# Attention with a compressive memory and an fp8 layer on one core: the order of the units in an even head, and the row tiles of the third strips

## The reference, cut to what matters

```python
# x: (2, 2048, 512); 4 query groups, 8 heads, 16 elements a head
x = layernorm(L0_attn_x)
q, k, v = x @ Wq.T, x @ Wk.T, x @ Wv.T
scores = einsum('bsqhd,bthd->bqhst', qh, kh) / sqrt(16)
a_dot = einsum('bqhst,bthd->bsqhd', softmax(scores), vh)
sigma_q = elu(q.reshape(b, s, 4, 128))
a_mem = sigma_q @ memory / (sigma_q @ memory_norm)
x1 = L0_attn_x + a_dot * (1 - w) + a_mem * w          # w = sigmoid(memory_weight)
out = x1 + fp8(layernorm(x1) / input_scale) * input_scale @ (weight * weight_scale).T
```

## Time and profile before

| | |
|---|---|
| median of 3 runs | 1942.49 us (1942.41 to 1942.53) |
| the profiled execution | 1942.58 us |
| span from its first to its last instruction | 1940.5 us |
| ACT busy | 1833.6 us, 94% of the span |
| PE busy | 1863.9 us, 96% |
| DVE busy | 1409.9 us, 73% |
| granted TensorE clock | 1.000 |

### The profile page before, as it was taken

The page is one execution under the profiler, slowest core; times in us unless marked ns, Lnnn a source line. Parts: engine busy times, 40 slices in busy tenths (PEclk is TensorE's granted clock), DMA queues, the critical chain, the costliest instruction groups (busy, mean ns, idle before and its releaser), DMA issues.

```text
span 1940.5 us, 115379 instructions
## 1 busy us (share of the span) xinstructions
PE 1863.9 (96%) x54988; PEld 1162.0 (60%) x54996; DVE 1409.9 (73%) x1833; ACT 1833.6 (94%) x1596; POOL 107.2 (6%) x150
## 2 busy tenths in 40 slices
PE   8999999999999999999999999999999999999998
PEld 7885555556565555555555555555655555555555
DVE  6675777777777777787777777777777777777755
ACT  5556999999999999999999999999999999999997
POOL 5541000000000000000000000000000000000000
PEclk9999999999999999999999999999999999999999
DMA  6654111121112211222112211212112211222111
GB/s 220 201 187 153 54 54 40 45 57 45 54 41 56 78 49 42 56 58 64 47 49 56 78 47 44 57 46 76 44 53 57 78 50 41 56 50 72 43 47 46
DMA packets 131327, 130.38 MB, mean 67 GB/s; under 512 B 30451, under 2 KB 106455, under 8 KB 130855
## 3 DMA queue, kind: packets, MB, share of 16 engines
q1 hardware_dynamic: 129847, 121.15, 21.2%
q10 hardware_dynamic: 1008, 1.84, 0.3%
HBM read 86.96 MB, written 32.24 MB: 61 GB/s over the span
## 4 chain that ended last, share of the span: by engine, by line
ACT 76%; PE 21%; issue 2%; DVE 1%; POOL 0%; DMA 0%; ACTq 0%; DVEq 0%; POOLq 0%
ACT pool L865 74%; PE ps L1153 8%; PE ps L945 6%; PE ps L1028 4%; ACT pool L872 1%; PE ps L1200 1%; PE ps L918 1%; DMA resid<-in_x 0%; PE ps L984 0%; POOL q_sq L727 0%; PE ps L909 0%; POOL xn L704 0%; PE ps L926 0%; DVE v_tiles L1608 0%; DVE v_tiles L1610 0%
## 5 line engine op out<-in xcount | busy, mean ns | idle before, releaser
L865 ACT ACTIVATE pool<-ps 128x1536 f32<-128x1536 f32 (+1 forms) x1388 | 1710.1, 1413 | 17.0 <-PE ps L1028 14.7
L1153 PE MATMUL ps<-pool,v_st 64*32 64x128 f32 (+2 forms) x35744 | 1398.3, 357 | 14.7 <-issue 13.7
L1153 PEld LDWEIGHTS ps<-pool,v_st 64*32 64x32 f32 x35744 | 854.5, 106 | 210.0 <-issue 54.3
L1028 PE MATMUL ps<-q_st,k_st 51*32 51x512 f16 x16128 | 903.6, 381 | 49.0 <-ACT pool L865 11.6
L1028 PEld LDWEIGHTS ps<-q_st,k_st 51*32 51x32 f16 x16128 | 246.0, 89 | 474.3 <-ACT pool L865 427.5
L1593 DVE TENSOR_SCALAR late<-ps 128x512 int32<-128x512 f32 x248 | 171.6, 692 | 212.5 <-PE ps L1028 212.5
L1608 DVE SCALAR_TENSOR_TENSOR v_tiles<-late 128x2048 f32<-128x2048 f32 x62 | 142.1, 2293 | 148.1 <-PE ps L1153 144.7
L1612 DVE SCALAR_TENSOR_TENSOR pool<-v_tiles,late 128x2048 f32<-128x2048 f32 x62 | 142.1, 2292 | 2.1
L1610 DVE SCALAR_TENSOR_TENSOR v_tiles<-v_tiles,late 128x2048 f32<-128x2048 f32 x62 | 142.1, 2292 | 2.1
L1603 DVE SCALAR_TENSOR_TENSOR late<-late 128x2048 f32<-128x2048 f32 x62 | 141.6, 2285 | 0.0
L747 POOL TENSOR_TENSOR rstd<-var_eps,minus_half 128x1 f32<-128x1 f32 x32 | 23.0, 720 | 1696.8 <-DVE var_eps L1672 1696.8
(11 more groups left out here) (169 smaller groups left out, 955.1 us busy)
## 6 DMA issues: line engine op xcount, KB each, us to landing
v_st<-v_aug SPq DMA_DIRECT2D x64, 256.0 KB, 3.5
q_st<-q_aug SPq DMA_DIRECT2D x127, 128.0 KB
k_st<-k_aug SPq DMA_DIRECT2D x127, 128.0 KB
sigma_kept<-y_out SPq DMA_DIRECT2D x32, 256.0 KB, 2.0
q_aug<-parts SPq DMA_DIRECT2D x32, 256.0 KB, 2.7
wqT<-sigma_kept SPq DMA_DIRECT2D x32, 256.0 KB, 3.8
q_st<-q_aug SPq DMA_DIRECT2D x127, 64.0 KB
k_st<-k_aug SPq DMA_DIRECT2D x127, 64.0 KB
```

The costliest lines, as they stand in the source:

```text
L865: act.activation(probs[:, u % HELD, 0:UNITS[u].width * CH], scored(u).rearrange("p a b -> p (a b)"), ACT.Exp, bias=LIFT, scale=EXP_UNIT / ...
L1028: return pe.matmul(ps[VW * c:VW * c + VW, bank, :], k_st[RT * r:RT * r + AUG, n % 2, keys:keys + VW], q_st[RT * r:RT * r + AUG, n % 2, q * ...
L1153: last = pe.matmul(acc[r][VW * c:VW * c + VW, :].rearrange("v (i s) -> v i s", s=VW)[:, places, :], v_st[rows, n % 2, j, :], by_place[rows ...
```

## The change

Three edits:

1. In an even head the two narrow units with the memory products move from places 0 and 2 to places 3 and 5. The head still has 22 units, 16 wide and 6 narrow, and its late units stay at places 10 to 13. The memory products now use the other third bank (odd units instead of even ones). `WEIGHED_LATER` stays as it was.
2. The row tile in which each half of a third strip runs now changes with every unit, instead of every second one.
3. VectorE takes and adds the sums of the head before first, and then adds both memory products.

```diff
-UNITS_OF_HEAD = (["2memory", "3", "2memory"] + ["3"] * 7 + ["2late"] * 4 + ["3"] * 8,
+UNITS_OF_HEAD = (["3", "3", "3", "2memory", "3", "2memory"] + ["3"] * 4 + ["2late"] * 4 + ["3"] * 8,
                  ["3", "3", "2product", "3", "2spare", "3", "3"] + ["2late"] * 4 + ["3"] * 11)
 WEIGH_BEHIND = 2
 WEIGHED_LATER = ((0, 1, 2), (0, 1, 2, 3, 9))
@@
             def third_scores(u, n, strip):
                 for c in range(P // VW):
-                    last = strip_scores(THIRD_BANK[u % SLOTS], n, strip, (c // 2 + u // 2) % ROW_TILES, c)
+                    last = strip_scores(THIRD_BANK[u % SLOTS], n, strip, (c // 2 + u) % ROW_TILES, c)
                 return last
@@
             def head(n):
                 g, h = divmod(n, HEADS)
+                if n > 0:
+                    take_sums(n - 1)
+                    add_sums(n - 1)
                 if n % 2 == 0:
                     add_memory(n)
-                if n > 0:
-                    take_sums(n - 1)
-                if n % 2 == 0:
                     add_memory(n + 1)
-                if n > 0:
-                    add_sums(n - 1)
                 if n % 2 == 0:
                     if g > 0:
                         tile_moments((g - 1) * TPC + h // 2)
```

## The result

The changed kernel takes 1969.91 us (median of four runs, 1963.16 to 1973.21) where the kernel before takes 1942.51 (four runs). The ratio is 1.0135, 95% interval 1.0107 to 1.0162. It is slower, by 27.4 us; the forecast was 1969.2 us. The profiled execution took 1969.06 us, of which 1967.0 are span.

A forecast was written before the change was run, and what follows sets the result against it. ScalarE was taken to set the pace, TensorE following with a small reserve. A net loss of 0.83 us in each of 32 even heads gives +26.6 us on 1942.58, other terms cancelling: 1969.1 to 1969.2 us, 8-in-10 range 1963 to 1975.

The forecast's parts named there:

- The path through turns 3 to 6: Even heads, unit 1's end to unit 6's end: TensorE's path takes 6.85 us where ScalarE alone needs 5.86.
- The losses: ScalarE's delay per even head: 0.14 us at unit 4 and 0.85 at unit 6, net 0.83 us a head.
- Unit 1's 0.16: Even heads of the kernel before: memory products at place 0 cost 0.16 us, 5.1 us in all, which the change removes.
- Edit 2: Third strips' row tiles: gain between nothing and 5.5 us where TensorE has fallen behind, taken as 1.5 us.
- The uncovered turns: Turns 3 to 6 without reserve: TensorE's stretches without visible cause cost up to 4.8 us there, taken as 1.5.
- The two terms of 1.5 us: The row-tile gain and the cost of unexplained TensorE stretches in turns 3 to 6, taken as cancelling.
- Edit 3: VectorE's new order: worth nothing, with covers of 0.5 us at the memory products' bank and 0.3 before the first late strip.
- The faster one: Rival, chance 0.05: TensorE is in time at unit 6, only the 0.16 us go away, 1937.4 us.
- Half of the loss is hidden: Rival, chance 0.04: only one of two delays comes through as turn 5's weighings overlap the memory products; 0.4 us a head, 1955 us.

The follow-up runs named there:

- experiment 6: Changed kernel with units 3 and 4 of even heads weighed one turn later, so turn 5 holds one weighing: 1949.58 us against 1935.18 for the kernel before, ratio 1.0072.
- experiment 7: Changed kernel with the second memory unit of even heads at place 7 instead of 5: 1989.03 us, ratio 1.0284 to the kernel before.
- experiment 1: Kernel before with only the third strips' row tiles changing every unit: 1938.28 us against 1938.9, ratio 0.9998.
- experiment 2: Changed kernel with the row-tile edit undone, the moved units and VectorE's new order kept: 1966.55 us, ratio 1.0140 to the kernel before.
- experiment 3: Changed kernel run again with nothing altered: 1963.77 us, ratio 1.0139 to the kernel before.
- experiment 10: Kernel before with third strips that never change their row tiles: 1943.65 us against 1942.81, ratio 1.0008.
- experiment 5: Changed kernel with VectorE's order put back to that of the kernel before: one run, 2087.78 us.
- experiment 8: Changed kernel with the second memory unit at place 7 and VectorE adding its product behind the fp8 layer's tile: 1966.86 us against 1942.81 for the kernel before, ratio 1.0123.

## Why the prediction was right

*The path through turns 3 to 6.* Forecast 6.85 us, measured 459.61 - 452.67 = 6.94. Step by step in head 10: 0.05 (0.05 forecast), 0.34 (0.34), 0.58 (0.58), weigh 0 0.67 (0.65), to the second memory products 1.44 (1.43), 0.57 (0.58), the two weighings 1.11 (1.10), scores 6 to their exponential 0.73 (0.67), 1.45 (1.45). The one step off by more than 0.02 is the last but one. I had taken it from place 1 of the kernel before; behind two weighings the tiles don't come free together, and the last matmuls of the third strip end 0.70 us after the first of the pair (457.43 to 458.13), where those of unit 4 end after 0.63 (454.31 to 454.94).

*The losses.* Unit 4: 0.14 forecast, 0.16 measured. Unit 6: 0.85 forecast, 0.91 measured. Unit 1's 0.16 is gone. Net a head 0.91, not 0.83. Over the 31 even heads from 2 on the steps give 28.1 us. The prediction counted head 0 as a loss of 0.83 us, and there it was wrong: that head became 1.0 us shorter. With the 0.5 us ahead of the first exponential this makes the 26.5 us by which the span grew. That the forecast's 26.6 us agree with it so closely is luck: 0.08 us a head too little and a head 0 that should not have been counted nearly cancel, and the kernel before changes by more than that from run to run. Experiments 6 and 7 split the 0.91 us. With one weighing in turn 5 0.43 are left, and with a wide unit and no memory products there nothing is left. So all of it needs the narrow unit with the memory products in turn 5, and half of it the second weighing beside them.

*Edit 2.* Put at 1.5 us of gain, between nothing and 5.5. Measured: nothing, within 2.5 us either way alone (experiment 1) and within some 4 us beside the others (experiments 2 and 3); with the opposite edit nothing either (experiment 10). The cause was argued rightly for the turns in which TensorE waits for ScalarE, where the median steps don't move by more than 0.005 us. The 1.5 us for the other turns is not confirmed, and not excluded. The rule weighed there from the Trainium skill (TensorE: Matmul & The Clock Gate, Step-by-step: what each phase is for), that matmuls stay in program order, would make edit 2 worth nothing, and the times agree with that. The rows don't: the split start of the scores (0.63 us for a block of eight in the earlier trace rows) is seen again after the change (455.20 to 455.81), and its first matmul at 455.20 starts ahead of one of the weighing before it, at 455.21. So the row tiles do run apart, and it still isn't worth anything that can be measured here.

*The uncovered turns.* Put at + 1.5 us. Units 6 and 7 of the changed kernel lose 1.0 us in all beyond 31 times the median, and those of the kernel before 1.2 us. So nothing was added there in these two profiles, and no run shows the 1.5 us. The two terms of 1.5 us that cancel in the forecast were both near nothing.

*Edit 3.* Put at nothing as long as its covers hold, and they held. VectorE was through with the first memory products' bank at 455.15, 0.60 us before the second products start at 455.75, where I had 0.5. And it stood idle 0.27 us before the first late strip, where I had 0.3:

```profile
454.54 0.61 DVE L1728 SCALAR_TENSOR_TENSOR resid<-ps,rnorm,resid 128x128 f32<-128x128 f32 x2
...
463.09 0.69 DVE L1593 TENSOR_SCALAR late<-ps 128x512 int32<-128x512 f32 x1 [0.27 <-PE ps L1028]
```

The second is the thinner one, and experiment 7 shows what lies behind it: with the memory unit two turns later, that cover is gone and costs 1.49 us in each of 27 heads. And edit 3 is needed for edit 1: without it weigh 0 waits 2.20 us, and the kernel takes 2088 us.

*The rivals.* The faster one needed the path to fall below 6.02 us, and it is 6.94. "Half of the loss is hidden" needed the weighings to overlap the memory products; they start 0.57 us behind them.

## What to carry to other kernels

Where two engines run in lockstep and the follower has a small reserve in each turn (here 1.16 us of work against 1.34), a list of work in turns is judged by each turn's own sum against the pace, carried over to the next turn. Totals of busy time don't show it: here those of the two engines moved by less than 4 us. Light work that is moved out of a turn with a little too much is only a gain if the turn that gets it has less: the same memory products cost nothing where nothing was weighed, 0.16 us beside one weighing (0.27 and 0.43 us where the turns just before had used up the reserve) and 0.9 beside two. The cheaper cure left the units where they were and moved a third of one weighing, 0.22 us, behind the next scores. Before moving a producer, count how late the last in its consumer's queue becomes.

## What the runs showed of the hardware

- The granted clock can fall to the 1.2 GHz level around one idle stretch of 2.2 us. In experiment 5 TensorE stood idle for 2.20 us in each even head from 2 on, in turns that were lightly filled (3.64 us busy of 6.70, the idle stretch included). In 28 of the 31 heads the clock then fell, for 3.4 us in 16 and for 6.8 us in 12 of them; in 18 it fell before TensorE began to work again and in 10 after. In heads 14, 22 and 62 it stayed at full speed behind the same stretch.
- It also fell behind full turns. In experiment 2 the clock fell to 0.50 for 3.4 us in an idle stretch of 2.33 us (660.87 to 663.21), though TensorE had been busy for 3.94 of the 4.00 us before. But the kernel before had 2.25 us of idle time at the same point of its work (655.97 to 658.22), behind 3.94 busy of 4.00 us too, and kept a clock of 1.00; so did experiment 8 through 2.54 us. What decides between the two is not shown here. In the main stage of the changed kernel the longest idle stretch was 1.75 us, and the clock stays at 1.000.
- What the low clock cost is read from experiment 5: 2.0 us a head on the mean over the three heads without it, of which unit 4's step shows 1.07 us (4.86 against 3.79, the median and the three heads).
- Eight score matmuls in eight tiles of the array take 0.41 us to the end of the last when TensorE comes from a wait, and 0.61 to 0.63 us behind a third strip and a weighing, where they start in pieces (455.20 to 455.44), as if the row tiles came free at different times.
